# A fused LayerNorm and graph convolution in float32: the order of the work before the first slots, and one row-block less ahead

## The chip, the cores and the metric

One core of one Trainium2 chip runs the whole kernel. The metric is the device time of one execution in microseconds. All data lie in HBM at the start, and the output is written back there.

## What is computed

N = 4096 rows, 256 features, everything float32:

```python
h   = relu((x - mean(x)) / sqrt(var(x) + 1e-5))      # per row of x, 4096 x 256
d   = where(rowsum(adj) > 0, rowsum(adj) ** -0.5, 0)  # adj is 4096 x 4096
out = x + relu((d[:, None] * adj * d[None, :]) @ h @ W + b)
```

The matrix adj is 64 MB, and the kernel reads it twice: once by rows for the row sums, once in a transposed order for the product.

## The kernel before

**Tiling.** TensorE computes the product transposed. h @ W is made first, without the factor 1/sqrt(var), in eight chunks of 4 tiles of 128 rows; chunks 0 to 4 (AHEAD = 5) before the main loop, chunks 5 to 7 inside it. A chunk goes: take_stats (L588, VectorE), means_of or mean_of (GpSimd), centre (L597, VectorE: subtract the mean, relu), turn (L775, TensorE transposes), a copy to SBUF (ScalarE), project (L791, TensorE), and then round_raw (L445, ScalarE) and rest_of_raw (L603, VectorE), which store the product in G as a rounded high part and a low rest in fp32r. Chunk 4 is projected in split form by project_parts (L809 to L811) after rest_of_turned.

**Main loop.** The transposed adj is cut into 64 slots of 1 MB. Slot g holds four tiles of 128 x 512. In the 14 steps k = 0 to 13 a step covers two tiles j = 2k, 2k + 1 of the contraction and eight output panels of 512, in four slots of two panels each; the last step k = 14 covers four tiles j = 28 to 31, one panel per slot (slots 56 to 63). For narrow slots round_slot (L411, ScalarE) makes hi = s[j] * at per half c, rounded to fp32r, and subtract (L652, VectorE) the rest lo, where s[j] = d * rstd of tile j; the wide slots are rounded as they are (L406, L656), and there s is multiplied into G by make_G (L638, L640, VectorE). I write hi(g, c) and lo(g, c). Both work two slots ahead of TensorE. multiply (L840 to L842) does three matmuls of 512 columns per tile and feature half: 24 per slot. A panel's PSUM pair is added into acc by gather (L668 in step 0, L671 later, VectorE) and is free then; there are two such pairs, and panels 0 and 1 stay in PSUM (HELD). In step 0 the panels come in the order 2 to 7, 0, 1.

**Row sums.** Row-block m is half of a tile of 128 rows of adj, 1 MB. sum_nat (L398, ScalarE) sums it; scale_of(j) (L549 to L557, GpSimd) needs blocks 2j and 2j + 1 and gives s[j]. Blocks 0 to 3 (EARLY = 4) are summed before the loop. nat_table says which blocks are loaded and summed in which slot: up to EARLY + min(2(g + 1), g + 4) + max(0, g - 20) // 8. With it block 63 lies in slot 52. scale_slots puts make_G(j) for j = 28 to 31 two slots behind the sum that it needs, at most in slot 55: j = 31 in slot 54.

**Order.** Each engine has its own program, written out by hand, and they meet at semaphores; an engine's instructions run in the order written. ScalarE does in slot g: round_slot(g + 2), the sums of NATS[g], and in the last step add_b. VectorE does the gathers of slot g and the subtractions of slot g + 2, then make_G of the slot; in the last step also scale_rows (L685) and finish (L699). Its calls before the loop:

```python
take_stats(0, first)
centre(0, first)
take_stats(0, second)
take_stats(1, first)
centre(0, second)
take_stats(1, second)
centre(1)
...
```

**Loads.** SyncE issues all DMAs on one queue: the halves of x chunk 0 (L346, L347), W (L348), chunk 1 (L309), chunks 2 to 4 with row-blocks 0 to 2 between them, block 3, slots 0 and 1, b; then per slot the row-blocks of NATS[g] (L339, each waits until the block four before it is summed) and the slot g + 3 (L343, waits until lo of slot g - 1 is made). In slot 55 it stores d (L327, waits for all of s), in slot 56 it spreads it over the partitions (L335), and in slot 57 it waits for G(31) and then issues four loads of transposed x (L361, L363), ahead of the loads of slots 60 to 63. After the loop it stores the output of position 0 to 7 (L382, L388) and loads the next x (L385) when a store has landed. add_b(pos) (L458) adds b to that x, and finish adds the result to it.

**Start.** TensorE runs WARM = 14 transposes of the identity into a PSUM pair (L853) before the first turn.

## Time and profile before

| what | value |
| --- | --- |
| median of 3 executions | 395.70 us (395.69 to 397.05) |
| the profiled execution's own time | 396.11 us |
| its span, first to last instruction | 394.3 us |
| TensorE busy | 383.9 us, 97% |
| VectorE busy | 319.9 us, 81% |
| ScalarE busy | 287.7 us, 73% |
| GpSimd busy | 117.2 us, 30% |
| DMA | 151.87 MB, mean 385 GB/s |
| mean granted TensorE clock | 0.997 |

The span and the profiled execution's time belong to the same execution; 1.8 us lie around the span. Busy times are unions of an engine's instructions. A load's time runs from its issue to its landing, so it holds the time that it stood in the queue.

### The profile page before, as it was taken

What the parts mean: (1) busy time and instruction counts of PE and PEld (TensorE: products, weight loads), DVE (VectorE), ACT (ScalarE), POOL (GpSimd) and SP (SyncE); (2) the same over time, 40 slices, a digit from 0 to 9 for tenths busy, and PEclk for the clock granted to TensorE, in tenths of its full rate; (3) what the DMA queues carried; (4) which work ended last, traced back from release to release, by engine and by line L of the source; (5) the groups of instructions that cost most, each with busy time, mean ns of one, the idle gap of its engine ahead of it and who ended that gap; (6) DMA issues with size and microseconds to landing.
All of it is one profiled execution on the core that took longest, in us unless ns stands there. A gap on an engine that the chain in (4) does not pass through costs nothing.

```text
span 394.3 us, 5160 instructions
## 1 busy us (share of the span) xinstructions
PE 383.9 (97%) x1750; PEld 318.4 (81%) x1750; DVE 319.9 (81%) x313; ACT 287.7 (73%) x283; POOL 117.2 (30%) x278
## 2 busy tenths in 40 slices
PE   6997999999999999999999999999999999999995
PEld 5885788888888888888888888888888888878884
DVE  4948958978686999959689995868889497899997
ACT  2789989888787778678977869787886777365531
POOL 2450675352121126213224831323323223000000
PEclk9999999999999999999999999999999999999998
DMA  8999999999999999999999999999999986898457
GB/s 283 423 421 418 420 421 421 419 422 423 412 421 421 418 421 421 416 422 421 418 421 421 421 415 422 416 419 423 421 419 412 408 310 218 318 369 325 135 190 262
DMA packets 24217, 151.87 MB, mean 385 GB/s; under 512 B 3328, under 2 KB 3328, under 8 KB 7552
## 3 DMA queue, kind: packets, MB, share of 16 engines
q1 hardware_dynamic: 24192, 151.55, 95.1%
q8 instruction: 14, 0.23, 0.2%
q14 instruction: 11, 0.09, 0.1%
HBM read 147.33 MB, written 4.22 MB: 384 GB/s over the span
## 4 chain that ended last, share of the span: by engine, by line
PE 83%; DMA 8%; DVE 3%; ACT 3%; issue 1%; SPq 1%; POOL 1%; DVEq 0%; ACTq 0%; POOLq 0%
PE moved L840 20%; PE moved L842 19%; PE moved L841 19%; PE held L840 6%; PE held L842 6%; PE held L841 6%; DMA out<-nat 3%; DMA out<-turned 3%; PE held L791 2%; DMA acc<-in_x 1%; DMA turned<-in_x_t 1%; ACT nat L398 1%; DVE lo L652 1%; PE moved L775 1%; PE moved L809 1%; PE moved L811 1%
## 5 line engine op out<-in xcount | busy, mean ns | idle before, releaser
L411 ACT ACTIVATE hi<-at,s 128x1024 fp32r<-128x1024 f32 x112 | 123.0, 1145 | 47.3 <-issue 32.4
L840 PE MATMUL moved<-hi,G 128*128 128x512 f32 x384 | 149.9, 390 | 2.6 <-DVE lo L652 1.2
L652 DVE SCALAR_TENSOR_TENSOR lo<-at,s,hi 128x1024 fp32r<-128x1024 f32 x112 | 141.0, 1278 | 12.5 <-ACT hi L411 12.5
L841 PE MATMUL moved<-lo,G 128*128 128x512 f32 x384 | 149.5, 389 | 0.0
L842 PE MATMUL moved<-hi,G 128*128 128x512 f32 x384 | 149.4, 389 | 0.0
L671 DVE TENSOR_TENSOR acc<-moved,acc 128x1024 f32<-128x1024 f32 x84 | 102.7, 1223 | 50.3 <-PE moved L842 50.0
L398 ACT ACTIVATE nat<-nat 128x2048 f32<-128x2048 f32 x64 | 122.0, 1908 | 6.0 <-DMA nat<-in_adj 5.9
L840 PEld LDWEIGHTS moved<-hi,G 128*128 128x128 f32 x384 | 72.1, 188 | 19.1 <-issue 2.9
L842 PEld LDWEIGHTS moved<-hi,G 128*128 128x128 f32 x384 | 72.1, 188 | 15.0
L841 PEld LDWEIGHTS moved<-lo,G 128*128 128x128 f32 x384 | 72.1, 188 | 14.9
L549 POOL TENSOR_TENSOR row_sum<-part 128x1 f32<-128x1 f32 x32 | 18.0, 562 | 182.5 <-ACT nat L398 182.5
L841 PE MATMUL held<-lo,G 128*128 128x512 f32 x128 | 49.8, 389 | 0.0
L840 PE MATMUL held<-hi,G 128*128 128x512 f32 x128 | 49.8, 389 | 0.0
L842 PE MATMUL held<-hi,G 128*128 128x512 f32 x128 | 49.8, 389 | 0.0
L406 ACT CAST hi<-at 128x2048 fp32r<-128x2048 f32 x8 | 15.3, 1915 | 19.8 <-PE moved L842 19.8
L842 PEld LDWEIGHTS held<-hi,G 128*128 128x128 f32 x128 | 24.0, 188 | 5.0
L841 PEld LDWEIGHTS held<-lo,G 128*128 128x128 f32 x128 | 24.0, 188 | 4.9
L840 PEld LDWEIGHTS held<-hi,G 128*128 128x128 f32 x128 | 24.0, 188 | 4.9
L557 POOL TENSOR_TENSOR s<-d,rstd 128x1 f32<-128x1 f32 x32 | 19.4, 608 | 2.5
L553 POOL TENSOR_TENSOR row_pow<-row_safe,minus_half 128x1 f32<-128x1 f32 x32 | 18.2, 567 | 2.7
L656 DVE TENSOR_TENSOR lo<-at,hi 128x2048 fp32r<-128x2048 f32 x8 | 18.2, 2284 | 0.0
L791 PE MATMUL held<-w_sb,turned 128*128 128x256 f32 x64 | 15.2, 383 | 1.0 <-ACT turned L422 0.8
(69 smaller groups left out, 246.3 us busy)
## 6 DMA issues: line engine op xcount, KB each, us to landing
nat<-in_adj SPq DMA_DIRECT2D x64, 1024.0 KB, 13.2
at<-in_adj_t SPq DMA_DIRECT2D x64, 1024.0 KB, 11.9
acc<-in_x SPq DMA_DIRECT2D x4, 512.0 KB, 7.6
nat<-d_dram SPq DMA_DIRECT2D x2, 1024.0 KB, 5.9
nat<-in_x_t SPq DMA_DIRECT2D x4, 512.0 KB, 4.1
turned<-in_x_t SPq DMA_DIRECT2D x4, 512.0 KB, 4.8
out<-nat SPq DMA_DIRECT2D x4, 512.0 KB, 4.9
turned<-in_x SPq DMA_DIRECT2D x3, 512.0 KB, 14.6
```

Of the source, the lines that this page charges most:

```text
L398: nc.scalar.activation(nat[m % LN][:, :], nat[m % LN][:, :], ACT.Copy, accum_out=part[:, m // 2, m % 2:m % 2 + 1]).then_inc(nat_summed, 1)
L411: nc.scalar.activation(hi[g % RING][:, 2 * c:2 * c + 2, :], at[g % LA][:, 2 * c:2 * c + 2, :], ACT.Copy, scale=s[:, j:j + 1]).then_inc(hi_ ...
L549: then(nc.gpsimd.tensor_tensor(out=row_sum[:, one], in0=part[:, j, 0:1], in1=part[:, j, 1:2], op=ALU.add))
L553: then(nc.gpsimd.tensor_tensor(out=row_pow[:, one], in0=row_safe[:, one], in1=minus_half[:, 0:1], op=ALU.pow))
L557: nc.gpsimd.tensor_tensor(out=s[:, one], in0=d[:, one], in1=rstd[:, one], op=ALU.mult).then_inc(s_ready, 1)
L652: nc.vector.scalar_tensor_tensor(out=lo[g % RING][:, tiles, :], in0=at[g % LA][:, tiles, :], scalar=s[:, j:j + 1], in1=hi[g % RING][:, til ...
L656: nc.vector.tensor_tensor(out=lo[g % RING][:, :, :], in0=at[g % LA][:, :, :], in1=hi[g % RING][:, :, :].bitcast(F32), op=ALU.subtract).the ...
L671: nc.vector.tensor_tensor(out=own, in0=pair[:, :, :], in1=own, op=ALU.add).then_inc(taken, 1)
L791: mm = nc.tensor.matmul(own, hT(c)[:, f, tile * P:(tile + 1) * P], w_sb[:, f, :], start=(f == 0), stop=(f == FD - 1))
L840: nc.tensor.matmul(into[:, f, :], big, hi[g % RING][:, t, :], start=begins, stop=False)
L841: nc.tensor.matmul(into[:, f, :], big, lo[g % RING][:, t, :], start=False, stop=False)
L842: mm = nc.tensor.matmul(into[:, f, :], small, hi[g % RING][:, t, :], start=False, stop=ends)
```

## The change

In seven places:
- SyncE no longer loads chunk 1; ScalarE issues that load as its first instruction.
- VectorE's order at the start: the statistics of chunk 0's second half, its centring, then all of chunk 1.
- Row-block 3 is summed on VectorE (sum_last_early, a reduce_sum) after centre(4), with a semaphore of its own; wait_summed waits for both. ScalarE's sum of it goes.
- ScalarE rounds slots 0 and 1 and then the raw products of chunks 3 and 4; before, the casts stood one after each slot. VectorE does rest_of_raw(3) behind the subtractions of slot 1 instead of ahead of them.
- TensorE does slot 0 by tiles: tile 0 for both panels, then tile 1 for both; before, panel by panel.
- nat_table has g + 3 for g + 4. From slot 2 on each row-block is loaded and summed one slot later or, where a slot has two blocks, one block later: block 63 in slot 53, and make_G(31) in slot 55.
- WARM is 16, and FILL = 5 transposes follow the first half of chunk 0.

```diff
--- before.py
+++ after.py
@@ -49,7 +49,9 @@
 
 FIRST_PART = 4
 
-WARM = 14
+WARM = 16
+
+FILL = 5
 
 
 def panel_order(k):
@@ -77,7 +79,7 @@
 
     table, m = [], EARLY
     for g in range(len(SLOTS)):
-        end = min(EARLY + min(2 * (g + 1), g + 4) + max(0, g - 20) // 8, 2 * NB)
+        end = min(EARLY + min(2 * (g + 1), g + 3) + max(0, g - 20) // 8, 2 * NB)
         table.append(range(m, end))
         m = end
     return table
@@ -248,6 +250,7 @@
         raw_hi_made = sem("raw_hi_made")
         raw_ready = sem("raw_ready")
         nat_summed = sem("nat_summed")
+        last_early_summed = sem("last_early_summed")
         s_ready = sem("s_ready")
         G_hi_made = sem("G_hi_made")
         G_ready = sem("G_ready")
@@ -297,6 +300,12 @@
         def G_count(j):
             return j - RAW * BW + 1
 
+        def wait_summed(eng, m):
+
+            eng.wait_ge(nat_summed, m + 1 if m < EARLY - 1 else m)
+            if m >= EARLY - 1:
+                eng.wait_ge(last_early_summed, 1)
+
         block = ctx.enter_context(nc.Block())
 
         @block.sync
@@ -335,7 +344,8 @@
                     sp.dma_start(nat[e][:, :], half.to_broadcast([P, HALF])).then_inc(d_row_landed[e], DMA)
 
             def load_nat(m):
-                at_least(sp, nat_summed, m - LN + 1)
+                if m >= LN:
+                    wait_summed(sp, m - LN)
                 sp.dma_start(nat[m % LN][:, :], adj_rows[m // 2, m % 2]).then_inc(nat_landed[m % LN], DMA)
 
             def load_slot(g):
@@ -346,7 +356,6 @@
             sp.dma_start(h(0)[:, 0:half, :], x[0][:, 0:half, :]).then_inc(x_first, DMA)
             sp.dma_start(h(0)[:, half:BW, :], x[0][:, half:BW, :]).then_inc(x_landed[0], DMA)
             sp.dma_start(w_sb[:, :, :], w).then_inc(w_landed, DMA)
-            load_x(1)
             for c in range(2, AHEAD):
                 load_x(c)
                 load_nat(c - 2)
@@ -357,7 +366,7 @@
             order = panel_order(LAST)
             for g, (k, q, _) in enumerate(SLOTS):
                 if k == LAST and q == 1:
-                    sp.wait_ge(nat_summed, 2 * NB)
+                    wait_summed(sp, 2 * NB - 1)
                     sp.wait_ge(G_ready, G_count(NB - 1))
                     for pos in range(LX):
                         sp.dma_start(x_out(pos), x_t[order[pos]]).then_inc(x_out_landed[pos], DMA)
@@ -458,6 +467,8 @@
                     nc.scalar.activation(x_out(pos)[:, f, :], x_out(pos)[:, f, :], ACT.Identity,
                                          bias=b_sb[:, f:f + 1]).then_inc(b_added, 1)
 
+
+            act.dma_start(h(1), x[1]).then_inc(x_landed[1], DMA)
             take_first_half()
             take_second_half()
             round_w()
@@ -473,10 +484,10 @@
                     take_high(c + 2)
                 if c >= 2:
                     sum_nat(c)
-            sum_nat(EARLY - 1)
+
             round_slot(0)
+            round_slot(1)
             round_raw(AHEAD - 2)
-            round_slot(1)
             round_raw(AHEAD - 1)
             for g, (k, q, _) in enumerate(SLOTS):
 
@@ -545,7 +556,7 @@
 
             def scale_of(j):
                 one = slice(j, j + 1)
-                pool.wait_ge(nat_summed, 2 * (j + 1))
+                wait_summed(pool, 2 * j + 1)
                 then(nc.gpsimd.tensor_tensor(out=row_sum[:, one], in0=part[:, j, 0:1], in1=part[:, j, 1:2],
                                              op=ALU.add))
                 nc.gpsimd.tensor_scalar(row_pos[:, one], row_sum[:, one], 0.0, None, ALU.is_gt)
@@ -596,6 +607,13 @@
                         dve.wait_ge(mean_ready, 2 * (j + at_once) // BW)
                     nc.vector.tensor_scalar(h(c)[:, t, :], h(c)[:, t, :], minus_mean[:, j:j + 1], 0.0,
                                             ALU.add, ALU.max).then_inc(h_ready, 1)
+
+            def sum_last_early():
+
+                m = EARLY - 1
+                dve.wait_ge(nat_landed[m % LN], DMA)
+                nc.vector.reduce_sum(part[:, m // 2, m % 2:m % 2 + 1], nat[m % LN][:, :],
+                                     axis=mybir.AxisListType.X).then_inc(last_early_summed, 1)
 
             def rest_of_raw(c):
                 dve.wait_ge(raw_hi_made, c + 1)
@@ -707,9 +725,8 @@
             take_stats(0, first)
             centre(0, first)
             take_stats(0, second)
-            take_stats(1, first)
             centre(0, second)
-            take_stats(1, second)
+            take_stats(1)
             centre(1)
             take_stats(2)
             centre(2)
@@ -719,13 +736,14 @@
                     rest_of_w()
                 rest_of_raw(c - 3)
                 centre(c)
+            sum_last_early()
             rest_of_raw(AHEAD - 3)
             rest_of_turned(AHEAD - 1)
             for c in range(2):
                 subtract(0, c)
-            rest_of_raw(AHEAD - 2)
             for c in range(2):
                 subtract(1, c)
+            rest_of_raw(AHEAD - 2)
             for g, (k, q, panels) in enumerate(SLOTS):
                 if NARROW[k] and NARROW[SLOTS[g + 2][0]]:
                     for p in range(2):
@@ -811,8 +829,10 @@
                         mm = nc.tensor.matmul(own, low, w_hi[:, f, :], start=False, stop=(f == FD - 1))
                 mm.then_inc(hW_done, 1)
 
-            def multiply(k, pos, i, g, p):
-                if i < HELD:
+            def multiply(k, pos, i, g, p, only=None):
+                if only is not None and only > 0:
+                    into = pair_of(("panel", k, i))
+                elif i < HELD:
                     into = held[i]
                     if k == 0:
 
@@ -822,7 +842,7 @@
                     pair_free(("panel", k, i))
                 n = len(SLOTS[g][2])
                 outer = [(c, f) for f in range(FD) for c in range(WIDTHS[k])] if (k, pos) == (LAST, NP - 1) else \
-                    [(c, f) for c in range(WIDTHS[k]) for f in range(FD)]
+                    [(c, f) for c in range(WIDTHS[k]) for f in range(FD) if only in (None, c)]
                 for c, f in outer:
                     j = FIRST[k] + c
                     t = c * n + p
@@ -845,13 +865,15 @@
                     if (pos, c, f) == (0, 0, FD - 1) and k in PROJECTING:
 
                         project_parts(PROJECTING[k])
-                if (k, pos) != (LAST, NP - 1):
+                if (k, pos) != (LAST, NP - 1) and only in (None, WIDTHS[k] - 1):
                     mm.then_inc(panel_done, 1)
 
             pe.wait_ge(consts_made, 1)
             for _ in range(WARM):
                 nc.tensor.transpose(moved[1][:, 0, 0:P], ident[:, :], ident[:, :])
             turn(0, range(BW // 2))
+            for _ in range(FILL):
+                nc.tensor.transpose(moved[1][:, 0, 0:P], ident[:, :], ident[:, :])
             pe.wait_ge(w_landed, DMA)
             project(0, range(1))
             turn(0, range(BW // 2, BW))
@@ -866,6 +888,12 @@
                 project(c, range(n, BW))
             project_parts(4)
             for g, (k, q, panels) in enumerate(SLOTS):
+                if g == 0:
+
+                    for c in range(WIDTHS[k]):
+                        for p, i in enumerate(panels):
+                            multiply(k, p, i, g, p, c)
+                    continue
                 for p, i in enumerate(panels):
                     pos = q * len(panels) + p
                     multiply(k, pos, i, g, p)
```

## Rows read from the trace of the kernel before

**Rows 1.** PE in two stretches: start:end length, busy (instructions), clock, DMA share, GB/s
```profile
43.45:389.80 346.35, 346.35 (x1560) 1.00 0.96 387
37.67:43.45 5.78, 5.74 (x24) 1.00 1.01 418
```

**Rows 2.** Timeline of PE, front: start, us, instruction, count, [idle before <-releaser]
```profile
1.67 3.25 PE L853 MATMUL moved<-ident 128*128 128x128 f32 x14 [1.67 <-POOL ident L510]
...
7.04 1.10 PE L791 MATMUL held<-w_sb,turned 128*128 128x256 f32 x4 [0.77 <-ACT turned L422]
...
8.61 0.70 PE L775 MATMUL moved<-ident,acc 128*128 128x128 f32 x4 [0.47 <-DVE acc L597]
...
43.45 0.50 PE L840 MATMUL moved<-hi,G 128*128 128x512 f32 x1
```

**Rows 3.** Timeline of VectorE (DVE), front
```profile
3.37 0.75 DVE L588 BATCH_NORM_STATS2 stats<-acc 128x6 f32<-128x256 f32 x2 [3.37 <-DMA acc<-in_x]
...
7.55 0.75 DVE L588 BATCH_NORM_STATS2 stats<-acc 128x6 f32<-128x256 f32 x2 [1.52 <-DMA acc<-in_x]
...
8.22 0.60 DVE L597 TENSOR_SCALAR acc<-acc,minus_mean 128x256 f32<-128x256 f32 x2
...
31.67 1.28 DVE L652 SCALAR_TENSOR_TENSOR lo<-at,s,hi 128x1024 fp32r<-128x1024 f32 x1 [1.53 <-ACT hi L411]
...
37.53 1.27 DVE L652 SCALAR_TENSOR_TENSOR lo<-at,s,hi 128x1024 fp32r<-128x1024 f32 x1
...
42.19 1.21 DVE L668 COPY acc<-moved 128x1024 f32<-128x1024 f32 x1
...
52.12 1.28 DVE L652 SCALAR_TENSOR_TENSOR lo<-at,s,hi 128x1024 fp32r<-128x1024 f32 x1 [1.35 <-ACT hi L411]
```

**Rows 4.** Timeline of ScalarE (ACT), front
```profile
23.87 1.92 ACT L398 ACTIVATE nat<-nat 128x2048 f32<-128x2048 f32 x1
...
30.49 1.15 ACT L411 ACTIVATE hi<-at,s 128x1024 fp32r<-128x1024 f32 x1 [1.67 <-POOL s L557]
```

**Rows 5.** Timeline of GpSimd (POOL), front: first and last instruction of s(1)
```profile
27.85 0.19 POOL L549 TENSOR_TENSOR row_sum<-part 128x1 f32<-128x1 f32 x1 [2.25 <-ACT nat L398]
...
30.26 0.19 POOL L557 TENSOR_TENSOR s<-d,rstd 128x1 f32<-128x1 f32 x1
```

**Rows 6.** Timeline of VectorE, end
```profile
344.35 0.48 DVE L640 SCALAR_TENSOR_TENSOR G<-turned,s,G 128x256 fp32r<-128x256 f32 x1
...
347.21 4.48 DVE L656 TENSOR_TENSOR lo<-at,hi 128x2048 fp32r<-128x2048 f32 x2
...
351.80 1.23 DVE L671 TENSOR_TENSOR acc<-moved,acc 128x1024 f32<-128x1024 f32 x1
...
355.77 2.29 DVE L656 TENSOR_TENSOR lo<-at,hi 128x2048 fp32r<-128x2048 f32 x1
...
391.05 0.75 DVE L699 SCALAR_TENSOR_TENSOR turned<-acc,minus_b,turned 128x512 f32<-128x512 f32 x1
```

**Rows 7.** The load of slot 2 on SyncE's queue, and its time to landing
```profile
L343 SPq DMA_DIRECT2D at<-in_adj_t x1: 435/435/435, 21.0 to 21.0; - x1
...
DMA to landing us min/median/max: 13.2/13.2/13.2
```

**Rows 8.** Waits of ScalarE: who <- releaser: us in total, times, longest
```profile
ACT hi L411 <- DMA at<-in_adj_t: 10.4, 15, 1.4
```

**Rows 9.** Timeline of SyncE's queue (SPq), end
```profile
344.91 0.81 SPq L363 DMA_DIRECT2D nat<-in_x_t  x2
```

**Rows 10.** Timeline of ScalarE, end
```profile
348.73 1.34 ACT L458 ACTIVATE nat<-nat,b_sb 128x512 f32<-128x512 f32 x2 [0.70 <-DMA nat<-in_x_t]
...
351.86 1.91 ACT L406 CAST hi<-at 128x2048 fp32r<-128x2048 f32 x1 [1.79 <-PE moved L842]
```

**Rows 11.** The chain that ended last, end: start, us, what
```profile
358.46 8.48 DMA out<-nat
...
383.28 3.98 DMA turned<-in_x_t
```

## The prediction

> **What bounds the kernel now.** I read the page for the busy shares, then the stretches, the timeline of each engine at both ends, and the chain that ended last. TensorE (PE) has no idle time between 43.45 and 389.80 us: 1560 matmuls in 346.35 us [rows 1], 0.227 us from one 512-column matmul to the next, 5.45 us for the 24 of a slot. So time can be won only where PE still waits, before 43.45 us, and only if what follows PE at the end moves with it. I name times on the clock of the trace of before throughout.
>
> In front, PE waits 0.47 us for VectorE's centred chunk 0 [rows 2]: VectorE reads the statistics of chunk 1 first, whose load landed just before 7.55 [rows 3]. Then slot 0's second tile waits for s(1). ScalarE sums row-blocks 2 and 3 one after the other from 23.87 on, 1.9 us each; the cast of hi(0,1) waits 1.67 us for s and starts at 30.49 [rows 4]; GpSimd's chain from row_sum to s runs 27.85 to 30.45 [rows 5]. From there VectorE sets the pace: lo(0,1) at 31.67, then without a gap a raw rest, two subtractions, a gather, lo(2,0) at 37.53, a gather, a subtraction, a raw rest, and the gather of slot 1 at 42.19 to 43.40 [rows 3], which frees the PSUM pair with which PE starts slot 2 at 43.45 [rows 2]. These ten pieces take 11.8 us, and I take the start of slot 2 as the mark of what the front gains.
>
> At the end the last worker is VectorE, not PE. PE's last matmul ends at 389.84, inside [rows 1], but VectorE works from 351.80 to 391.80 with no idle row; its slot takes 6.12 us (lo of slot 59 at 355.77, four pieces per slot) against PE's 5.45 [rows 6]. Whatever VectorE loses after 351.80 is lost at the end.
>
> **The front, step by step.** *VectorE's order.* Centring the second half of chunk 0 no longer stands behind chunk 1's load. Its statistics can start at 5.3, after which comes GpSimd's mean (some 0.7), so it starts near 6.75 instead of 8.22 [rows 3]. PE turns it as soon as it has projected tile 0, at 8.0 instead of 8.61 [rows 2]; the copy behind that shift and chunk 1's four statistics then put project(1) some 0.9 us earlier. From there to slot 0 PE is nearly gapless, so ScalarE's sum of row-block 2 goes from 23.87 to about 22.95.
> *The sum of row-block 3 on VectorE.* There is no such reduction in the trace. The nearest row by shape, 128x2048 with two inputs, takes 2.28 us (two in 4.48, [rows 6]); by work, statistics of 256 columns take 0.375 (two in 0.75, [rows 3]), eight of them 3.0. I take 2.3, from about 21.3, when its load lands, to 23.6. VectorE was idle for most of that, and the two rests behind it become 0.3 us late at most (1.0 at 3.0 us), so the split product of chunk 4 ends near 28.8. PE can use that: slot 0's first tile of both panels, 12 matmuls or 2.7 us, runs to 31.5 while s(1) is made.
> *s(1).* Both sums are there at 25.0; with 2.6 us on GpSimd [rows 5] s(1) comes at 27.6, hi(0,1) ends at 28.8, lo(0,1) starts there, 2.9 us before 31.67.
> *Slots 0 and 1 ahead of the two casts; raw rest 3 after slot 1's subtractions.* The ten pieces stay ten, in another order, and none is removed before slot 2's mark. With that alone slot 2 would start 2.9 us earlier.
> *What is late next.* lo(2,0) needs the load of slot 2, issued at 21.0 and landed 13.2 us later, at 34.2 [rows 7], behind a queue of loads that the change leaves in this order. The DMA engines were busy all along. With 1.15 us of cast, lo(2,0) can't start before 35.4, where before it started at 37.53 [rows 3]. That caps the gain at 2.1 us. Chunk 1 from ScalarE's queue adds no bytes; its issue (about 0.4 us) lies before ScalarE's first need of its table, and the next issues of SP move up by as much, which may bring later landings 0.3 forward. **Front: -2.1**, between -1.8 and -2.4.
> *WARM 16 and FILL 5.* The 14 warm-up transposes took 3.25 us from 1.67 on, 0.23 each, so two more may hold the first turn by up to 0.2; five more, about 1.1 us, fall before PE's first projection at 7.04, for which it waited 0.77 after the last turn had drained [rows 2]. I take 0 for both: that wait covers them, and without it they would cost 0.2 to 0.3 where PE isn't yet what slot 2 waits for.
>
> **The middle.** nat_table now loads and sums one row-block later from slot 2 on. For slots 4k the sum that s(2k+1) needs comes directly before the rounding, so ScalarE waits for GpSimd's 2.6 us each fourth slot. That is covered: ScalarE and VectorE work two slots ahead. The tightest place is slot 4: its second lo starts at 52.12 before [rows 3], and PE wants it near 55.8, or 53.8 with the front shorter; I get 51.1 to 52.4 for its end. The slot loads, for which ScalarE waited 10.4 us in 15 places [rows 8], land one 1 MB load earlier, 2.5 us, which pays for the 2.1 us by which PE is ahead. Cost 0.
>
> **The end.** This is the part that the change's title doesn't speak of. With one row-block later, row-block 63 is summed in slot 53, not 52, and scale_slots puts make_G(31) into slot 55, not 54. There it stands behind lo of slot 57. Before, its second instruction ran from 344.35 to 344.83; now the pair comes after the first of the two 128x2048 subtractions that start at 347.21, so from 349.4 to 350.3 [rows 6], 5.44 us later relative to everything else. Two things hang on it. PE needs G(31) with matmul 18 of slot 56, at 350.24: at most 0.2 us, and PE has 0.4 to spare at the end. And SyncE waits for it before it issues the four transposed-x loads, which started at 344.91, right behind it [rows 9]. They go to 350.35. ScalarE's adding of b at position 0, at 348.73 on the landing, goes to 354.2 and ends at 355.5; the cast of slot 59 stands behind it in order, at 355.5 to 357.4 instead of 351.86 [rows 10]; so lo of slot 59 starts at 357.4 instead of 355.77: VectorE loses **1.6 us**, from which nothing gets it back, since its last row starts at 391.05 [rows 6] in one unbroken run. Behind that the loads and stores at the end, which SyncE does one after the other, from the store at 358.46 to the load at 383.28 [rows 11], move by some 3.4 us: 1.6 for the subtraction they wait for, the rest from four slot loads still in the queue. The last x lands at 387.26, half of its addition of b takes 0.7 [rows 10], and VectorE wants that half two pieces of 0.7 before its last row (391.05, [rows 6]), at 389.67: 1.65 us of air; it needs 3.4 - 1.6 = 1.8, so 0.15 more. **End: +1.7.**
>
> The sum on this execution is 396.11 - 2.1 + 1.7 = 395.7. Its time stands 0.4 above the median of 395.70, so I predict 395.3.
>
> **A rule against the order of the loads.** The rows show that the engines are busy from the first packet and that chunk 0's first half is used at 3.37, chunk 1 at 7.55 [rows 3]; which of two queues goes first no row shows. A 512 KB load at the 418 GB/s of [rows 1] takes 1.25 us: by bounds, chunk 0 is late by 0 to 1.25. I take 0.4. The Trainium skill, DMA: Bandwidth & Descriptors, section Queues, rings and completion order, says that each DMA engine alternates between the queues that have work. By that rule chunk 0 would pay nearly the whole 1.25, which is rival 3; no run here shows yet whether it holds.
>
> **Rivals.**
> 1. *The end costs nothing* (the cast of slot 59 gets ahead, or VectorE makes up). Then the front's gain stands alone: 393.6, 2.1 under the median. For it: PE is gapless up to 389.8. Against it: no idle row of VectorE after 351.80.
> 2. *Loads and stores become the end.* The whole 5.44 us reaches the last load of x, and only its 1.65 us of air cover it: +3.8 at the end, -2.1 in front, 397.4, slower than before. It decides as soon as the chain of stores moves by over 3.2 us; I put it at 3.4, so it is near. Against it: part of 5.44 is absorbed where SyncE waits for subtractions anyway.
> 3. *Chunk 1 delays chunk 0.* With 1.25 us on the first load PE's first turns are late; project(1) comes 0.4 late instead of 0.9 early, lo(0,1) at 29.8, slot 2 at 41.6: the front gains 1.85, or 1.0 if a PE pause costs it more. 395.5 to 396.4.
>
> **Chances.** Forecast 0.5; rival 1 0.2; rival 2 0.15; rival 3 0.15. A measurement here can tell 0.5%, 2.0 us, from no change. Rival 1 at 393.6 lies on that edge, and the front may be worth 0.3 more: 0.2 for faster. Slower by 2.0 us wants rival 2 and a poorer front: 0.06. The range leaves out half of rival 1's low side and the worst of rival 2: 393.5 to 397.1.
>
> **What would show it.** Right: slot 2 starts near 41.35, with lo(2,0) right behind its cast and the cast on the landing; the 128x2048 cast of slot 59 behind ScalarE's additions of b for position 0; VectorE unbroken to the end, and about 1.6 us more between slot 56 and the end. Wrong: a span 2 us shorter with the additions of b at their old distance from the end; ScalarE waits over 3 us at slots 4k with PE idle after 41 us; or PE's first turn later than 5.5.

## The result and the profile after

The changed kernel took 397.94 us (median of 18, 396.41 to 399.37) against 396.78 for the kernel before in the same measurement (18 executions, 395.51 to 397.22): ratio 1.0032, interval 1.0019 to 1.0046. It is slower by about 1.2 us, where I forecast a gain of 0.4 and a range up to 397.1 around a before of 395.7. Of the 2.6 us between the forecast of 395.3 and 397.94, 1.1 is the kernel before, which measures 396.78 here; the other 1.5 is the change, which went the other way than forecast. Its profiled execution took 396.65 us with a span of 394.8, only 0.5 over the one before; that difference between profile and median is part of the story. Both kernels have two groups of times in this measurement: the one before 8 executions at 395.5 to 396.3 and 10 at 396.7 to 397.2, the changed one 7 at 396.4 to 397.1 and 11 at 397.85 to 399.4. So it is slower by about 1.0 in the lower group and 1.5 in the upper. In a later measurement the same kernel took 399.08 (6 executions), ratio 1.0070.

I read the profile after from both ends, as the one before. TensorE (PE), front:

```profile
1.67 3.67 PE L873 MATMUL moved<-ident 128*128 128x128 f32 x16 [1.67 <-POOL ident L521]
...
6.83 0.70 PE L793 MATMUL moved<-ident,acc 128*128 128x128 f32 x4 [1.49 <-DVE acc L608]
...
8.30 1.10 PE L809 MATMUL held<-w_sb,turned 128*128 128x256 f32 x4 [0.22 <-ACT turned L431]
...
36.30 0.50 PE L860 MATMUL moved<-hi,G 128*128 128x512 f32 x1 [1.16 <-DVE acc L686]
...
42.09 0.50 PE L860 MATMUL moved<-hi,G 128*128 128x512 f32 x1
```

The first turn comes at 6.83, not 5.16; PE idles 1.49 us before it, although two warm-up transposes more were run. The projection of tile 0 follows at 8.30, where it was at 7.04 [rows 2]. Slot 1 waits 1.16 us for a gather, and slot 2 starts at 42.09: 1.36 us before the old 43.45 [rows 2], not 2.1. VectorE, front:

```profile
5.04 0.75 DVE L599 BATCH_NORM_STATS2 stats<-acc 128x6 f32<-128x256 f32 x2 [5.04 <-DMA acc<-in_x]
...
21.90 2.28 DVE L615 TENSOR_REDUCE part<-nat 128x1 f32<-128x2048 f32 x1
...
30.30 3.68 DVE L670 SCALAR_TENSOR_TENSOR lo<-at,s,hi 128x1024 fp32r<-128x1024 f32 x3 [1.53 <-ACT hi L420]
...
36.16 1.27 DVE L670 SCALAR_TENSOR_TENSOR lo<-at,s,hi 128x1024 fp32r<-128x1024 f32 x1
```

ScalarE, front: the sum of row-block 2, and the cast that waits for s(1):

```profile
24.39 1.92 ACT L407 ACTIVATE nat<-nat 128x2048 f32<-128x2048 f32 x1
...
29.11 3.23 ACT L420 ACTIVATE hi<-at,s 128x1024 fp32r<-128x1024 f32 x3 [1.67 <-POOL s L568]
```

Chunk 0's first half is there at 5.04 instead of 3.37 [rows 3]. The new sum takes 2.28 us, as its two-input neighbour did [rows 6]. Slot 0's second lo starts at 30.30, 1.37 before the old one [rows 3]; lo(2,0) at 36.16, again 1.37. So here the front is not held by the load of slot 2, as I thought, but still by s(1). The later of its two sums is now that of row-block 2: it starts at 24.39, 0.52 later than before [rows 4], where I had it 0.9 earlier. One sum less ahead of s(1) gains 1.9 us, and 0.52 of that is lost again.

The end, first SyncE and ScalarE:

```profile
348.98 0.81 SPq L372 DMA_DIRECT2D nat<-in_x_t  x2
```

```profile
352.31 1.34 ACT L467 ACTIVATE nat<-nat,b_sb 128x512 f32<-128x512 f32 x2 [5.67 <-DMA nat<-in_x_t]
...
353.55 1.90 ACT L415 CAST hi<-at 128x2048 fp32r<-128x2048 f32 x1
...
389.21 1.33 ACT L467 ACTIVATE turned<-turned,b_sb 128x512 f32<-128x512 f32 x2 [3.95 <-DMA turned<-in_x_t]
```

The four loads of x start at 348.98 instead of 344.91 [rows 9]; on a clock that starts with slot 56 (344.63 here, 346.02 before) that is 5.46 us later. The addition of b at position 0 waits 5.67 us for them, and the cast of slot 59 stands behind it at 353.55, where it was at 351.86 [rows 10] although PE is 1.4 us ahead. VectorE and the chain that ended last:

```profile
348.40 0.49 DVE L658 SCALAR_TENSOR_TENSOR G<-turned,s,G 128x256 fp32r<-128x256 f32 x1
...
348.80 2.28 DVE L674 TENSOR_TENSOR lo<-at,hi 128x2048 fp32r<-128x2048 f32 x1
...
355.49 2.29 DVE L674 TENSOR_TENSOR lo<-at,hi 128x2048 fp32r<-128x2048 f32 x1 [0.43 <-ACT hi L415]
...
390.04 0.75 DVE L717 SCALAR_TENSOR_TENSOR turned<-acc,minus_b,turned 128x512 f32<-128x512 f32 x1 [0.69 <-ACT turned L467]
...
391.42 0.75 DVE L717 SCALAR_TENSOR_TENSOR turned<-acc,minus_b,turned 128x512 f32<-128x512 f32 x1
```

The chain:

```profile
358.18 10.85 DMA out<-nat
...
385.16 4.03 DMA turned<-in_x_t
```

The make_G(31) that ends at 348.89 stands between lo of slots 57 and 58; lo of slot 59 waits 0.43 us for the cast. Near the end there is a new idle row, 0.69 us before the finish at 390.04: VectorE waits for the last addition of b, ScalarE for the last load of x, and that for the chain of stores, whose first takes 10.85 us instead of 8.48 [rows 11]. VectorE's last finish is at 391.42 instead of 391.05 [rows 6]: 0.37 later in all, which is -1.38 from the front and +1.75 at the end (from the start of slot 56 on). Of the 1.75, 1.1 are lost up to lo of slot 59 and 0.65 behind it.

### The profile page after: what moved, and what is told of

Its sections match the earlier page's. It is cut to its first block, busy times and chain, and to the rows that moved or that the text cites. A ratio compares the mean times of both kernels' runs of the same rounds, so it can differ in the third digit from the quotient of the medians.

```text
span 394.8 us, 5261 instructions
## 1 busy us (share of the span) xinstructions
PE 383.9 (97%) x1757; PEld 319.0 (81%) x1757; DVE 322.3 (82%) x314; ACT 284.4 (72%) x281; POOL 123.3 (31%) x278
## 4 chain that ended last, share of the span: by engine, by line
PE 82%; DMA 9%; DVE 4%; ACT 2%; issue 1%; POOL 1%; SPq 0%; DVEq 0%; POOLq 0%; ACTq 0%
PE moved L860 19%; PE moved L862 19%; PE moved L861 19%; PE held L860 6%; PE held L861 6%; PE held L862 6%; DMA out<-nat 4%; PE held L809 3%; DMA out<-turned 3%; DVE lo L674 1%; DMA acc<-in_x 1%; DMA turned<-in_x_t 1%; PE moved L793 1%; DVE lo L670 1%; DMA nat<-in_x_t 1%
## 5 line engine op out<-in xcount | busy, mean ns | idle before, releaser
L407 ACT ACTIVATE nat<-nat 128x2048 f32<-128x2048 f32 x63 | 119.9, 1904 | 0.5 <-DMA nat<-in_adj 0.5
L560 POOL TENSOR_TENSOR row_sum<-part 128x1 f32<-128x1 f32 x32 | 20.6, 645 | 176.9 <-ACT nat L407 176.8
L568 POOL TENSOR_TENSOR s<-d,rstd 128x1 f32<-128x1 f32 x32 | 24.8, 774 | 2.5
L564 POOL TENSOR_TENSOR row_pow<-row_safe,minus_half 128x1 f32<-128x1 f32 x32 | 19.1, 596 | 2.7
```

Of the source, the lines that this page charges most:

```text
L407: nc.scalar.activation(nat[m % LN][:, :], nat[m % LN][:, :], ACT.Copy, accum_out=part[:, m // 2, m % 2:m % 2 + 1]).then_inc(nat_summed, 1)
L560: then(nc.gpsimd.tensor_tensor(out=row_sum[:, one], in0=part[:, j, 0:1], in1=part[:, j, 1:2], op=ALU.add))
L564: then(nc.gpsimd.tensor_tensor(out=row_pow[:, one], in0=row_safe[:, one], in1=minus_half[:, 0:1], op=ALU.pow))
L568: nc.gpsimd.tensor_tensor(out=s[:, one], in0=d[:, one], in1=rstd[:, one], op=ALU.mult).then_inc(s_ready, 1)
```

## The experiments

All times are medians; "both edits" below is experiment 3. I name kernels by their experiment. Experiments 1 to 4, 5 to 8, 9 to 12 and 13 to 15 ran on one chip each, where the kernel before took 396.39, 396.20, 396.55 and 396.65 us; between two of these groups the ratios to the kernel before compare better than the times.

**1. make_G back in slot 54.** In the changed kernel:

```diff
-                table.setdefault(min(g + 2, last), []).append(m // 2)
+                table.setdefault(min(g + 1, last), []).append(m // 2)
```

> The changed kernel with one edit: scale_slots puts make_G one slot behind its sum instead of two, so make_G(31) is back in slot 54. My theory (front gains 1.4, end loses 1.75, by the make_G that holds the four loads of x): the front stays (slot 2 starts near 42.1), the four loads of x start near 343.5, VectorE ends near 390.4, the span is about 393.0 and the time 1.4 us under the kernel before. Rival (the end is lost because the row-blocks come later, through the later d or a DMA queue that is fuller at the end): the span stays near 394.8 and the time 0.4 to 1.2 over the kernel before.

396.05 us (11), ratio to before 0.9990 (0.9978 to 1.0003); the changed kernel in the same measurement took 399.08. SyncE issues the loads of x at 344.86, and VectorE has no idle row after 350 us: 3 us between the medians, 2.5 between the two spans, for one number in a table (it moves make_G of j = 28 to 30 too, for which no load waits). The end is as expected. The front is not: PE's timeline,

```profile
6.94 1.12 PE L793 MATMUL moved<-ident,acc 128*128 128x128 f32 x4 [1.59 <-DVE acc L608]
...
43.39 0.50 PE L860 MATMUL moved<-hi,G 128*128 128x512 f32 x1
```

has slot 2 at 43.39, not 42.1, though the front's code is that of the changed kernel. The span is 394.3, not 393.0.

**2. Chunk 1 by SyncE again.**

```diff
+            load_x(1)
             for c in range(2, AHEAD):
...
-            act.dma_start(h(1), x[1]).then_inc(x_landed[1], DMA)
```

> The changed kernel with chunk 1 loaded by SyncE again. My theory (chunk 1 on a second queue shares the DMA engines with chunk 0's first half, which landed at 5.01 instead of 3.35): chunk 0 lands near 3.35 again, TensorE's first turn is near 5.4, slot 2 starts near 41.35 with the load of slot 2 (34.1) as the limit, the time falls 0.7 under the changed kernel, to about 0.2 to 0.5 over the kernel before. Rival (the front is held by the sum on VectorE or by GpSimd, not by chunk 0): slot 2 stays near 42.1 and the time stays.

396.85 us (11), ratio 1.0012 (1.0002 to 1.0022). Chunk 0's first half lands at 3.30, the first turn is at 5.14 and slot 2 at 41.54. It gains 2.2 us on the changed kernel of this measurement, more than the 0.7 expected: that kernel's slot 2 starts at 43.57 (experiment 4), not at 42.09. But in its profiled execution the end is as late as in the changed kernel (last finish at 391.59 against 391.42): VectorE waits there 0.86 us for the cast of slot 59, which stands behind an addition of b, and 0.95 for the last addition. So the front's further gain did not all get through the chain of loads and stores.

**3. Both edits.** The diffs of experiments 1 and 2 together.

> Both edits at once: make_G one slot earlier, chunk 1 by SyncE. My theory: the gains add, slot 2 near 41.35 and the end as in the kernel before: 2.1 us under the kernel before, near 394.7 against 396.8. Rival: if something else takes the end (the load of slot 2 or the chain of stores), under 1.4.

394.08 us (5; 393.98 to 394.40), ratio 0.9948 (0.9934 to 0.9962). PE's timeline, and the load of slot 2 with its time to landing:

```profile
5.20 0.70 PE L793 MATMUL moved<-ident,acc 128*128 128x128 f32 x4
...
6.67 1.10 PE L809 MATMUL held<-w_sb,turned 128*128 128x256 f32 x4 [0.22 <-ACT turned L432]
...
41.09 0.50 PE L860 MATMUL moved<-hi,G 128*128 128x512 f32 x1 [0.41 <-DVE acc L686]
```

```profile
L353 SPq DMA_DIRECT2D at<-in_adj_t x1: 434/434/434, 19.9 to 19.9; - x1
...
DMA to landing us min/median/max: 14.0/14.0/14.0
```

First turn at 5.20, slot 2 at 41.09, 2.36 us earlier than before, and all of it but 0.2 reaches the end (span 392.2 against 394.3). The load of slot 2 is issued at 19.9 and lands 14.0 later, at 33.95. In the seven profiles where chunk 1 comes by SyncE, row-block 3 is summed on VectorE and the clock is at its upper level by 7.6 us, slot 2 starts 7.13 to 7.14 us after this landing, wherever that lies between 33.90 and 35.23. This limit, which I had put down for the changed kernel, is real, but only these kernels reach it.

**4. The changed kernel once more.**

> The changed kernel itself once more, for a second profile. The first profile shows 0.5 us more than before, while the medians show 1.2. My theory: the loads and stores of the last slots land later in most executions than in the one profiled, so this profile has either the same end as the first (span near 394.8) or a longer one in which the first store takes over 10.9 us and the last addition of b holds VectorE for more than 0.7. Rival: the spread lies in the front or the middle, and TensorE's slots start later there by 0.5 to 1.

399.08 us (6). My theory of a later end was mostly wrong and the rival mostly right: of the 1.95 us between the spans of the two profiles 1.5 lie ahead of slot 2 and 0.5 behind the start of slot 56. What the front shows is the clock. PE's timeline, and the stretches of PE (start:end length, busy, granted clock, DMA):

```profile
6.96 0.70 PE L793 MATMUL moved<-ident,acc 128*128 128x128 f32 x4 [1.95 <-DVE acc L608]
...
8.42 2.05 PE L809 MATMUL held<-w_sb,turned 128*128 128x256 f32 x4
...
43.57 0.50 PE L860 MATMUL moved<-hi,G 128*128 128x512 f32 x1
```

```profile
8.00:10.00 2.00, 1.92 (x6) 0.50 0.98 412
...
10.00:12.00 2.00, 2.00 (x10) 0.67 1.04 428
```

The same program, with a pause of 1.95 us before the first turn. The granted clock falls to its lower level (0.50: 1.2 GHz of 2.4) between 7.9 and 11.3, and the four matmuls of tile 0's projection take 2.05 us instead of 1.10. Slot 2 starts at 43.57, 1.5 us later than in the first profile, and of the front's gain nothing is left. In experiment 1 the record of the clock begins at the upper level only at 10.4, and its matmuls up to 10.2 have the lower level's pitch, 0.43 us for 256 columns instead of 0.22: the same loss.

**5. Only make_G late, in the kernel before** (make_G(31) in slot 55; those of j = 28 to 30 move too).

```diff
-                table.setdefault(min(g + 2, last), []).append(m // 2)
+                table.setdefault(min(g + 3, last), []).append(m // 2)
```

> The kernel before with one edit: scale_slots puts make_G three slots behind its sum, at most in slot 55, so make_G(31) stands in slot 55 behind the lo of slot 57 as in the changed kernel; loads and sums stay. My theory (the end is lost by this alone): the front is unchanged (slot 2 at 43.45), the four loads of x are issued near 350.3 instead of 344.9, and the kernel is 1.7 to 2.9 us slower than before. Rival (the row-blocks themselves, one later, cost the end): under 0.5 slower.

398.87 us (5), ratio 1.0056 (1.0037 to 1.0076): 2.2 us by the ratio, 2.7 between the medians. The front is untouched (slot 2 at 43.49), the loads of x go from 344.91 to 350.35, exactly the time that the prediction had worked out. VectorE's two new idle rows:

```profile
357.39 2.29 DVE L656 TENSOR_TENSOR lo<-at,hi 128x2048 fp32r<-128x2048 f32 x1 [0.90 <-ACT hi L406]
...
391.78 0.75 DVE L699 SCALAR_TENSOR_TENSOR turned<-acc,minus_b,turned 128x512 f32<-128x512 f32 x1 [0.55 <-ACT turned L458]
```

**6. Only chunk 1 on ScalarE's queue, in the kernel before.**

```diff
-            load_x(1)
...
+            act.dma_start(h(1), x[1]).then_inc(x_landed[1], DMA)
             take_first_half()
```

> The kernel before with only the load of chunk 1 moved to ScalarE's queue. My theory: chunk 0's first half lands at 5.0 to 5.5 instead of 3.35, TensorE idles 1.5 to 2 us before its first turn at 6.9, and in the executions in which the granted clock falls to the lower level within the next microseconds (or rises to the upper one only near 10) slot 2 starts 1.3 us later than in those in which it stays; slower than before by 0.5 to 2.5 us, with a spread over 1 us. Rival (the second queue only shifts what VectorE has in hand): within 0.5 of before with the old spread.

399.34 us (6; 398.45 to 399.69), ratio 1.0068 (1.0049 to 1.0087): 2.7 us slower, 3.1 between the medians, more than the 0.5 to 2.5 expected.

```profile
6.91 1.12 PE L775 MATMUL moved<-ident,acc 128*128 128x128 f32 x4 [2.00 <-DVE acc L597]
...
8.79 2.05 PE L791 MATMUL held<-w_sb,turned 128*128 128x256 f32 x4 [0.77 <-ACT turned L421]
...
46.36 0.50 PE L840 MATMUL moved<-hi,G 128*128 128x512 f32 x1
```

A pause of 2.00 us before the first turn, the projection of tile 0 in 2.05 us, and slot 2 at 46.36, 2.9 later. The clock is at its upper level only from 12.8. The shortest of these executions is longer than the longest of the kernel before in this measurement (398.09). They spread over 1.2 us, as expected, but none is as short as one in which the clock stayed up would be.

**7. A longer warm-up, in the changed kernel.**

```diff
-WARM = 16
+WARM = 26
```

> The changed kernel with WARM = 26, so that TensorE's warm-up reaches to the late first turn near 6.9. My theory (the other half of the front's loss, and its spread, is the clock that TensorE's pause costs): TensorE's pause before the first turn is under 0.5, the granted clock is full from about 5.5 on in the profile, slot 2 starts near 42.1 as in the changed kernel's first profile, and the time is 0.7 to 1.5 under the changed kernel's 399.08 of this chip, with a spread under 1 us. Rival (the late chunk alone): no change against 399.1, slot 2 near 43.5.

398.36 us (7; 397.90 to 399.53), ratio 1.0050. PE has no pause before the first turn, the clock is up from 7.0 and slot 2 starts at 42.35; yet only 0.7 us come out against 399.08 (0.8 by the ratios). In the profile VectorE waits 0.78 us for the cast of slot 59 and 1.48 for the last addition of b, and from slot 56 on it takes 3.2 us more than in the kernel before. The late loads of x hide what the front gains. (This profiled execution is the longest of the seven, with 3.0 us around its span instead of 1.8.)

**8. Row-block 3 summed on ScalarE, in both edits.**

```diff
+            m = EARLY - 1
+            act.wait_ge(nat_landed[m % LN], DMA)
+            nc.scalar.activation(nat[m % LN][:, :], nat[m % LN][:, :], ACT.Copy,
+                                 accum_out=part[:, m // 2, m % 2:m % 2 + 1]).then_inc(last_early_summed, 1)
             round_slot(0)
...
-            sum_last_early()
```

> The kernel with both edits (394.08) with the sum of row-block 3 on ScalarE again, behind the sum of row-block 2. My theory (s(1) is what releases slot 0's second tile, and the sum on VectorE brings it 1.9 forward): s(1) comes 1.9 us later, lo(0,1) near 30.7 to 31.2, slot 2 near 42.5, 1.4 to 1.9 slower than with both edits. Rival (the load of slot 2 at 34.0 limits anyway): under 0.5 slower.

395.28 us (10), ratio 0.9969, 1.2 us slower than both edits (0.8 by the ratios, 1.4 to 1.9 expected); slot 2 at 42.71 with the load of slot 2 at 34.37, which alone would allow 41.51. The sum on VectorE is worth this much; the rest of its 1.9 us was covered by the load.

**9. Slot 0 panel by panel, in both edits.**

```diff
-                if g == 0:
-
-                    for c in range(WIDTHS[k]):
-                        for p, i in enumerate(panels):
-                            multiply(k, p, i, g, p, c)
-                    continue
```

> The kernel with both edits with slot 0 panel by panel again. My theory: tile 0 of panel 2 (6 matmuls) is then all that TensorE can do before lo(0,1) near 29, so it waits about there by up to 0.5; the first panel is complete earlier, but the chain over VectorE to slot 2 is the same, so slot 2 moves by under 0.3 and the time by under 0.3. Rival (the order by tiles carries part of the front's gain): 0.5 or more slower.

394.04 us (5), slot 2 at 41.04, as my theory had it. The order by tiles is worth nothing measurable here.

**10. The old warm-up and no fill, in both edits.**

```diff
-WARM = 16
+WARM = 14
...
-FILL = 5
+FILL = 0
```

> The kernel with both edits with WARM = 14 and FILL = 0. My theory: TensorE's pauses in the first 8 us are then those of the kernel before, where the clock rose at 6.4 and stayed, so the time is within 0.3 of both edits (394.08). Rival (the fill keeps the clock up): the granted clock rises later or falls back within the first 12 us and the time is 0.5 to 1.5 higher, with a spread.

394.97 us (10; 393.87 to 395.19), 0.9 slower and spread over 1.3 us. The rival is right: in its profile the clock is at the upper level only from 10.3, although PE's pauses are those of the kernel before, whose clock rose at 6.4. The fill isn't free decoration, or the two warm-up transposes more aren't: the edit takes both away and doesn't separate them.

**11 and 12. The old table of row-blocks; the first two loads of x without the wait.**

```diff
-        end = min(EARLY + min(2 * (g + 1), g + 3) + max(0, g - 20) // 8, 2 * NB)
+        end = min(EARLY + min(2 * (g + 1), g + 4) + max(0, g - 20) // 8, 2 * NB)
```

```diff
                     wait_summed(sp, 2 * NB - 1)
-                    sp.wait_ge(G_ready, G_count(NB - 1))
                     for pos in range(LX):
+                        if pos == 2:
+                            sp.wait_ge(G_ready, G_count(NB - 1))
```

> The kernel with both edits with the row-blocks in their old slots (g + 4) and make_G two slots behind, as before. My theory: with TensorE 2.3 us ahead of before the loads of 1 MB more in front still come in time, so the time is within 0.4 of both edits. Rival (the later row-blocks pay for the shorter front): TensorE waits somewhere in slots 4 to 12 and the time is over 0.7 higher.

> The kernel with both edits, and SyncE issues the first two loads of transposed x without waiting for G(31), which only the third and fourth need. My theory: with make_G(31) in slot 54 the end is bound by VectorE's unbroken work, not by these loads, so nothing is gained: within 0.3 of 394.08. Rival (the chain of loads and stores still holds the end): 0.5 to 1.5 faster.

The first, with make_G two slots behind its sum as before: 394.97 us (10), 0.9 slower. In its profile the load of slot 2 landed at 35.23, and ScalarE's cast waited for it:

```profile
35.26 2.19 ACT L421 ACTIVATE hi<-at,s 128x1024 fp32r<-128x1024 f32 x2 [2.33 <-DMA at<-in_adj_t]
```

so 14 repeats it. The second: 393.97 us (6), no different from both edits; with make_G in slot 54 SyncE's wait costs nothing.

**13. The first experiment with WARM = 26.**

> The changed kernel with make_G one slot earlier (the first experiment, 396.05, whose clock rose only at 10.4) and WARM = 26. My theory (chunk 1 on the second queue costs the front 0.7 by late data and 1.3 by the clock): the clock is full from about 7, slot 2 starts near 42.3, the span is about 393.2, the time 1.0 to 1.3 under the first experiment, near 395.0, and 0.9 to 1.2 over the kernel with both edits. Rival (the late data cost all of it): no change against 396.05.

394.95 us (9), ratio 0.9963, 1.1 under experiment 1, as expected.

```profile
1.67 4.99 PE L873 MATMUL moved<-ident 128*128 128x128 f32 x26 [1.67 <-POOL ident L521]
...
7.89 1.10 PE L809 MATMUL held<-w_sb,turned 128*128 128x256 f32 x4 [0.22 <-ACT turned L431]
...
41.68 0.50 PE L860 MATMUL moved<-hi,G 128*128 128x512 f32 x1
```

Chunk 0's first half still lands late (4.61, though 0.5 earlier than in experiment 1), but PE runs transposes up to the turn, the clock is up from 5.7, and slot 2 starts at 41.68. What remains to both edits is 0.9.

**14 and 15. Experiments 11 and 3 again, on one chip.**

> The kernel e11 once more: both edits, but row-blocks as before (g + 4). Theory A (the old table makes slot loads land 2.5 us later, which TensorE now feels in slots 5 to 8): slot 8 minus slot 2 is 33.4 as in e11 instead of 32.8, and it is 0.5 to 0.9 slower than both edits also where the load of slot 2 lands at 34.0. Theory B (only the late landing of slot 2's load in that execution): slot 8 minus slot 2 is 32.8 and the time is within 0.2 of both edits.

> The kernel with both edits once more, beside the two others: 394.1, slot 2 starts 7.14 us after the load of slot 2 has landed, as in the profiles of four kernels so far. Rival: a slot 2 that is not bound to that landing.

394.81 (6) and 394.08 us (6). The edit of 14 is that of 11, with 15 beside it. This time the loads of slot 2 landed alike (34.36 and 34.59), and slot 2 started at 41.49 and 41.73. The old table then loses from slot 2 to slot 8, 33.9 us instead of 32.8, and 1.0 of it lies in slot 6. The load of slot 7 lands at 63.45 instead of 60.72, the cast of slot 7 waits for it, lo of slot 7 for the cast, and the gather for which PE waits in slot 6 stands behind that lo. ScalarE's and PE's rows:

```profile
63.47 2.19 ACT L421 ACTIVATE hi<-at,s 128x1024 fp32r<-128x1024 f32 x2 [0.48 <-DMA at<-in_adj_t]
```

```profile
63.56 0.50 PE L860 MATMUL moved<-hi,G 128*128 128x512 f32 x1
...
67.13 0.50 PE L860 MATMUL moved<-hi,G 128*128 128x512 f32 x1 [0.56 <-DVE acc L689]
```

Two parts of the change have no experiment of their own: VectorE's order at the start, and the casts of slots 0 and 1 ahead of the raw products.

## Why the prediction was wrong

*The end was right in mechanism; its size in the first profile is partly luck.* make_G(31) in slot 55, the loads of x 5.4 us late, the addition of b ahead of the cast of slot 59: each is in the profile, and experiments 1 and 5 show that this alone costs the end. I had 1.7 us, measured from slot 56 to the last finish. The profiled execution has 1.75, but that is the least of the five profiles with make_G(31) in slot 55: experiment 5 has 2.1 (2.2 by the ratio, 2.7 between the medians), the second profile of the changed kernel 2.2, experiment 2 2.45 and experiment 7 3.2. What VectorE loses up to lo of slot 59 is right: I had 1.6, and it is 1.1 in the first profile, 1.45 to 1.6 in the others. The term that was short is the chain of loads and stores. I gave it 0.15 us beyond that; it is 0.65 in the first profile and 0.5 to 1.75 in the others. So 1.75 came out as 1.1 + 0.65, where the sum had 1.6 + 0.15. I had the first store take 10.3 us (8.48 + 3.4 - 1.6); it took 10.6 to 10.9, and 11.8 in experiment 7, and the last load of x became the end. Rival 2 was the right mechanism there, at 1.75 to 3.2 of its 3.8 us.

*The failed step is "I take 0.4" for chunk 0.* The prediction bounded it by 0 and 1.25 us; it was 1.7 in the first profile, 1.7 to 1.9 in experiments 1, 4, 6 and 7, and 1.3 in experiment 13. Both loads, issued within 10 ns of each other, land within 0.5 us of each other, each near 5, so neither goes first. That agrees with the rule of the Trainium skill that I had weighed (DMA: Bandwidth & Descriptors, Queues, rings and completion order: a DMA engine alternates between the queues that have work). By that rule I had estimated a price of nearly 1.25 us, and took a third of it. The bound of 1.25 was itself too low. It took the DMA engines to run at 418 GB/s throughout, on the claim that they are busy from the first packet, for which no row was shown. The traces have them at less than half of that rate where the two queues start together. Between 2 and 3 us, first the kernel before, then the changed one (the last two numbers of a row are the DMA engines' share and GB/s):

```profile
2.00:3.00 1.00, 1.00 (x6) 1.00 (x5) 0.00 (x0) 0.00 (x0) 0.00 (x0) 1.00 0.99 338
...
2.00:3.00 1.00, 1.00 (x6) 1.00 (x5) 0.00 (x0) 0.43 (x1) 0.00 (x0) 1.00 0.54 158
```

All six profiles with chunk 1 on ScalarE's queue have 145 to 190 GB/s there, all eleven with SyncE's queue alone 324 to 371. Why the start is slower is open. With chunk 0 late, the sum of row-block 2 started at 24.39 instead of the 22.95 of the prediction, and the front gained 1.36 us, not 2.1. PE's first turn at 6.83 is past the 5.5 that the prediction named as a sign of being wrong. Rival 3 happened; its slot 2 at 41.6 was still 0.5 too early, and its time of at most 396.4 too low.

*The step that was missing is the clock.* "I take 0 for both", of WARM and FILL, covered only the transposes' own time. The late chunk leaves PE idle for 1.5 to 2.0 us before the first turn, and in the second profile the granted clock then fell for 3.4 us, at 1.3 to 1.5 us for slot 2. Of two profiles of the same program one shows it (43.57) and one doesn't (42.09). That likely makes the two groups of the changed kernel's times, which lie 1.7 apart, but it is not shown: two of its executions are profiled, one of each kind. The kernel before has two groups as well, 1.3 apart, of which no profile shows the upper one; that its clock varies too is seen only in experiment 5, whose front is the same, with the record at the upper level from 4.7 instead of 6.4. Experiment 13 separates pause and late data: without the pause slot 2 is at 41.7, 1.7 before experiment 1, and the median is 1.1 better. In its profile chunk 0 also landed 0.5 earlier, so some 1.2 us of the 1.7 are the pause with its clock.

*Right in the front:* the reduction's 2.3 us; s(1) as what releases slot 0 (experiment 8); the load of slot 2 as the next limit at 2.1 us, reached only with chunk 1 on SyncE's queue, where both edits have 41.09 and 41.73 against my 41.35, and lo(0,1) at 28.7 to 29.0 against my 28.8. *Wrong in the middle:* I gave the later row-blocks nothing. They are worth 0.7 us (experiments 14 and 15), since the 2.7 us by which they bring the load of slot 7 forward are needed as soon as the front is shorter. That is no error of the sum, which had this as a cover, but it says that the part of the change that spoils the end also serves the middle, and the remedy is to move make_G, not the loads.

In sum: forecast -2.1 + 1.7; the profiled execution -1.38 + 1.75; with the clock lost, in the second profile, +0.1 + 2.2. The median of 397.94 lies between these two executions, 396.65 and 398.62. Why all six executions of the later measurement are over 398.4, while 7 of the first 18 are under 397.2, is open. The best kernel here is both edits: 394.08 us, 2.3 to 2.6 faster than the kernel before (ratio 0.9939, interval 0.9923 to 0.9955 in the repeat) and 3.9 to 5.0 under the change as it was made (397.94 and 399.08).

## What to carry to other kernels

When a table shifts one stage, follow every other table that is worked out from it: here one row-block later moved a small instruction past a big one, and a wait for it held four loads and with them the end. The first load that the critical engine needs should have the DMA engines to itself: a second queue beside it cost it 1.3 to 1.9 us here. And when a load is made later by a microsecond, ask what TensorE does in that time: a pause in the start costs its own length and then may cost the clock, so a few idle transposes that reach to the first real one can be worth more than their place suggests (1.1 us from experiment 1 to 13).

## What I had not expected of the hardware

- Two loads issued at 0.718 and 0.724 us on two queues, 512 and 256 KB, landed at 5.19 and 5.01, where the smaller one alone at the head had landed at 3.35. The small one paid 1.66 us, more than the 1.25 that the whole large one takes at 418 GB/s, and between 2 and 3 us the DMA engines moved 158 GB/s instead of 338.
- The granted clock in the first 13 us differs between executions of one program: its record begins at the upper level at 5.6 and stays, or falls again from 7.9 to 11.3 (the changed kernel); with the same pauses it begins at 6.4 (before) or 10.3 (experiment 10). At the lower level a 256-column float32 matmul pass comes every 0.427 us, at the upper every 0.216.
- In one execution (experiment 11) the 1 MB load ahead of slot 2's landed 4.1 us behind its predecessor instead of 2.5 (experiment 3). The load of slot 2 came 1.28 us later than there, and slot 2 started 1.28 us later.
